# Experts' low-rank output in two float32r passes, with the feed-forward's vector steps in a new order

## The reference

```python
RANKS = (8, 16, 32, 64); TOPK = 1; SCALING = 1.0 / 4
base = x @ W.T + b                      # W [512, 512]
gate = x @ gate_w.T + gate_b            # 4 logits; the best of the four ranks is chosen
lora = (x @ A.T)                        # A [64, 512]; the columns up to the chosen rank are kept
x = _layernorm(x + base + lora_kept @ B.T)   # B [512, 64]
```

## Time and profile before

| | |
|---|---|
| Median of three runs | 645.35 us |
| The profiled execution's own time | 645.23 us |
| Its span | 643.1 us, so 2.1 us lie around it |
| Granted clock of PE | 0.998 |
| Busy: PE, DVE, ACT, POOL | 632.0, 396.3, 381.6, 65.0 us |

### The profile page before, as it was taken

One profiled execution on the slowest core, in us unless ns is written; L12 is line 12 of the kernel. 1 busy time (PEld: TensorE's weight loads), 2 busy tenths in 40 slices (PEclk: granted clock), 3 DMA queues, 4 the chain that ended last, 5 costly groups with the idle time before them and its releaser, 6 DMA issues.

```text
span 643.1 us, 8521 instructions
## 1 busy us (share of the span) xinstructions
PE 632.0 (98%) x3226; PEld 470.0 (73%) x3226; DVE 396.3 (62%) x633; ACT 381.6 (59%) x527; POOL 65.0 (10%) x116
## 2 busy tenths in 40 slices
PE   9999999999999999999999999999999999999996
PEld 6655555544558888888888888887777888888874
DVE  4798787667988777767667355335655212125467
ACT  2977789976987697576675154223565343316532
POOL 1032142311330000000000000001211000000012
PEclk9999999999999999999999999999999999999999
DMA  7771585512253134233320003056010322100002
GB/s 246 288 243 52 188 268 172 162 52 92 81 152 120 39 110 139 73 104 111 94 83 2 1 1 131 1 216 274 1 33 2 115 77 88 33 1 0 1 33 99
DMA packets 25590, 63.92 MB, mean 99 GB/s; under 512 B 5541, under 2 KB 10725, under 8 KB 24782
## 3 DMA queue, kind: packets, MB, share of 16 engines
q1 hardware_dynamic: 23294, 61.68, 29.4%
q10 hardware_dynamic: 2256, 1.70, 0.8%
HBM read 58.77 MB, written 4.60 MB: 99 GB/s over the span
## 4 chain that ended last, share of the span: by engine, by line
PE 88%; DVE 4%; ACT 4%; DMA 1%; issue 1%; SPq 1%; POOL 0%; POOLq 0%; DVEq 0%; ACTq 0%
PE bank L1043 18%; PE bank L1031 8%; PE bank L1030 8%; PE bank L1032 8%; PE bank L1122 8%; PE bank L1121 8%; PE bank L882 4%; PE bank L802 3%; PE bank L606 3%; PE bank L741 2%; PE bank L1097 1%; DMA codes<-in_c_qkv 1%; PE bank L912 1%; PE bank L926 1%; PE bank L984 1%
## 5 line engine op out<-in xcount | busy, mean ns | idle before, releaser
L1232 ACT ACTIVATE line<-line 128x1024 f32<-128x1024 f32 x87 | 91.4, 1050 | 0.2
L1030 PE MATMUL bank<-xh,wh 128*128 128x512 f32 x224 | 87.5, 391 | 0.0
L1031 PE MATMUL bank<-xl,wh 128*128 128x512 f32 x224 | 87.5, 391 | 0.0
L1032 PE MATMUL bank<-xh,wl 128*128 128x512 f32 x224 | 87.3, 390 | 0.0
L1043 PE MATMUL bank<-wh,xh 128*128 128x512 f32 x192 | 76.1, 396 | 0.2 <-DVE xl L2128 0.2
L1043 PE MATMUL bank<-wh,xl 128*128 128x512 f32 x192 | 74.9, 390 | 0.0
L2211 DVE SCALAR_TENSOR_TENSOR arena<-bank,ff_s,arena 128x512 f32<-128x512 f32 x28 | 21.0, 752 | 72.9 <-PE bank L1122 63.8
L2128 DVE TENSOR_TENSOR xl<-arena,xh 128x1024 fp32r<-128x1024 f32 (+1 forms) x26 | 29.7, 1141 | 35.4 <-ACT xh L1536 35.3
L1121 PE MATMUL bank<-xh,wh 128*128 128x512 f32 x128 | 50.3, 393 | 0.0
L1536 ACT ACTIVATE xh<-arena 128x1024 fp32r<-128x1024 f32 (+1 forms) x26 | 25.6, 991 | 41.3 <-PE bank L1043 34.8
L1122 PE MATMUL bank<-xl,wh 128*128 128x512 f32 x128 | 49.9, 390 | 0.0
(11 more groups left out here) (219 smaller groups left out, 1264.3 us busy)
## 6 DMA issues: line engine op xcount, KB each, us to landing
codes<-in_c_gu SPq DMA_DIRECT2D x14, 512.0 KB, 3.8
scales<-in_s_gu SPq DMA_DIRECT2D x28, 256.0 KB, 4.0
codes<-in_t_gu SPq DMA_DIRECT2D x8, 512.0 KB, 4.2
codes<-in_c_dn SPq DMA_DIRECT2D x7, 512.0 KB, 4.6
scales<-in_s_dn SPq DMA_DIRECT2D x14, 256.0 KB, 3.9
fold<-in_t_dn SPq DMA_DIRECT2D x1, 3584.0 KB, 15.7
codes<-in_c_qkv SPq DMA_DIRECT2D x6, 512.0 KB, 4.8
scales<-in_t_gu SPq DMA_DIRECT2D x6, 512.0 KB, 3.8
```

The costliest lines, as they stand in the source:

```text
L1030: pe.matmul(dst, wh[:, s, c:c + P], xh[:, k, cols], start=(k == 0), stop=False)
L1031: pe.matmul(dst, wh[:, s, c:c + P], xl[:, k, cols], start=False, stop=False)
L1032: last = pe.matmul(dst, wl[:, s, c:c + P], xh[:, k, cols], start=False, stop=(k == KD - 1))
L1232: nc.scalar.activation(below(slot), below(slot), ACT.Prelu, bias=bias, scale=scale, alpha=alpha).then_inc(bent, 1)
```

## The change

`lora_out` is two float32r products in place of one float32 product. The first has 128 rows: the stationary operand `lm_both` holds the low parts of the 64 masked columns in rows 0 to 63 and their high parts in rows 64 to 127, and `b_both` holds B's high part in rows 0 to 63 and B's low part in rows 64 to 127. The second has 97 rows: the high parts against B's high part, and two rows of ones against b's high and low parts. Its ones are written once on ACT.

For that `choose` makes two more DVE instructions: a copy of the masked columns to float32r (the high part) and a subtraction (the low part), each of 128x64, and each waits for the one before it. `lora_T` turns 128 columns, and `lora_T_out` is two ACT instructions (128x128 and 64x128) in place of one of 64x128. B and b come as two tiles (`b_two`, 256 KB, and `b_one`, 97 rows) in place of `bT0` (130 KB); they are loaded later, in SP's loop at t = 4. ACT rounds them once (`experts_high`), and DVE makes their low rows once (`experts_low`, two instructions between `choose(0)` and `choose(1)`).

The steps are in a new order. On DVE a step is now: the `add_lora`s, part 0 of the units, the wait and `ln_head` of tile t, `choose` of tile t+2, `m_low_of`, `x_low` of tile t-2, then part 1 of the units. On ACT `lora_T_out` of tile t+1 stands behind `x_T_out` in step t, ahead of part 1 of the units, where that of tile t stood first in step t.

```diff
             def lora_out(b):
                 pe.wait_ge(lmT_ready, b + 1)
-                pe.matmul(bank[FF_BANK[b % 3]][:, :], lmT[0:RMAX + 1, b % 2, :], bT0[0:RMAX + 1, :], start=False, stop=True).then_inc(f0_ps, 1)
+                if b == 0:
+                    pe.wait_ge(lm_ready, 2)
+                pe.matmul(bank[FF_BANK[b % 3]][:, :], lm_both[:, b % 2, :], b_both, start=False, stop=False)
+                pe.matmul(bank[FF_BANK[b % 3]][:, :], lm_one[0:ONE_ROWS.stop, b % 2, :], b_high_one[0:ONE_ROWS.stop, :], start=False, stop=True).then_inc(f0_ps, 1)
...
-                nc.scalar.activation(lmT[0:RMAX, b % 2, :], turn_bank(b)[0:RMAX, P:2 * P], ACT.Copy).then_inc(lmT_ready, 1)
+                nc.scalar.activation(lm_both[:, b % 2, :], turn_bank(b)[:, P:2 * P], ACT.Copy)
+                nc.scalar.activation(lm_one[0:RMAX, b % 2, :], turn_bank(b)[RMAX:P, P:2 * P], ACT.Copy).then_inc(lmT_ready, 1)
...
-                nc.vector.tensor_tensor(lm[:, s, :].rearrange("p (r m) -> p r m", m=SEG), ps[:, 0:RMAX].rearrange("p (r m) -> p r m", m=SEG),
-                                        mask.unsqueeze(1).to_broadcast([P, RMAX // SEG, SEG]), ALU.mult).then_inc(lm_ready, 1)
+                chosen, high = lm[:, s, 0:RMAX], lm_high[:, s, RMAX:P]
+                link(nc.vector.tensor_tensor(chosen.rearrange("p (r m) -> p r m", m=SEG), ps[:, 0:RMAX].rearrange("p (r m) -> p r m", m=SEG),
+                                             mask.unsqueeze(1).to_broadcast([P, RMAX // SEG, SEG]), ALU.mult))
+                link(nc.vector.tensor_copy(high, chosen))
+                nc.vector.tensor_tensor(chosen, chosen, f32(high), ALU.subtract).then_inc(lm_ready, 1)
...
             for t in range(NT):
-                if t >= 3:
-                    x_low(2 * NT + t - 3)
...
                 if t == 4:
                     down_stack_low()
+                dve.wait_ge(f0_ps, t + 1)
+                ln_head(2 * NT + t, plus(FF_BANK[t % 3]))
                 if t + 2 < NT:
                     choose(t + 2)
                 if FIRST_M <= t < FIRST_M + KD:
                     m_low_of(t - FIRST_M)
-                dve.wait_ge(f0_ps, t + 1)
-                ln_head(2 * NT + t, plus(FF_BANK[t % 3]))
+                if t >= 2:
+                    x_low(2 * NT + t - 2)
```

More of the change, by code:

```diff
@@ L170, in decoder_kernel @@
         ad_st = sb("ad_st", [STACK, FF], F32R)
+        with nc.sbuf_tensor("lm_one", [P, T], F32R) as lm_one:
+            pass
         folded_m = sb("folded", [P, T])
@@ L188, in decoder_kernel @@
         gate_v = sb("gate_v", [P, 2, NL + 3 * SEG])
-        lmT = sb("lmT", [P, 2, P])
-        probT = lmT
+        with nc.sbuf_tensor("lm_both", [P, 2, P], F32R) as lm_both:
+            pass
+        probT = sb("probT", [P, 2, P])
         prob = sb("prob", [P, 2, P])
@@ L221, in decoder_kernel @@
         bT_d, at = carve(arena, at, D)
+        b_high_at = at
         wk2, at = carve(arena, at, D)
@@ L237, in decoder_kernel @@
         lora_l = wo0
+        b_two, b_one = wk3, m_free[:, 0:D]
+        b_both, b_high_one = arena_r[:, b_low_at:b_low_at + D], arena_r[:, b_high_at:b_high_at + D]
+        ONE_ROWS = slice(RMAX, RMAX + ROWG + 1)
+        lm_one = lm_one[:, 0:2 * P].rearrange("p (s t) -> p s t", s=2)
         ad_high = wh[:, :, :].rearrange("p s c -> p (s c)")[:, 0:FF]
@@ L546, in _ @@
                     load_codes(C_O + 1 + t // 2)
+                if t == KD:
+                    sp.dma_start(b_two, i["b_two"]).then_inc(in_ffn0, 16)
+                    sp.dma_start(b_one[0:ONE_ROWS.stop, :], i["b_one"]).then_inc(in_ffn0, 16)
             load_scales(C_O + NT // 2)
@@ L1384, in _, with experts_high @@
             unit_bends(NT, 1)
+            def experts_high():
+                act.wait_ge(in_ffn0, 64)
+                nc.scalar.activation(b_both, b_two, ACT.Copy)
+                nc.scalar.activation(b_high_one[0:ONE_ROWS.stop, :], b_one[0:ONE_ROWS.stop, :], ACT.Copy).then_inc(stack_hi, 1)
             for t in range(1, NT + 2):
+                if t == NT + 1:
+                    experts_high()
                 if 2 <= t < NT:
@@ L1459, in _ @@
                     m_high_of(t - FIRST_M)
-                for u, h in half_plan(3, t, 1):
-                    unit_bends(u, h)
-                if t == 1:
+                if t == 2:
                     for n in range(2):
@@ L1466, in _ @@
                     x_T_out(2 * NT + t - 2, dst=xh)
+                if t + 1 < NT:
+                    lora_T_out(t + 1)
+                for u, h in half_plan(3, t, 1):
+                    unit_bends(u, h)
                 if t < 2:
@@ L2009, in _ @@
             turn_norm(2 * NT - 1)
+            experts_low()
             choose(1)
@@ L2304, in layout @@
         "w0T": rows(c(f["L0_ffn_W"].T)), "agT": rows(np.concatenate([f["L0_ffn_A"][rank_at].T, np.stack([gate_w[n] for n in LOGITS], 1)], 1)),
-        "bT0": np.concatenate([f["L0_ffn_B"].T[rank_at], f["L0_ffn_b"][None]]), "g_b": np.array([[gate_b[n] for n in LOGITS]], np.float32),
+        "b_two": np.concatenate([f["L0_ffn_B"].T[rank_at]] * 2),
+        "b_one": np.concatenate([f["L0_ffn_B"].T[rank_at], f["L0_ffn_b"][None], np.zeros((ROWG - 1, D), np.float32), f["L0_ffn_b"][None]]), "g_b": np.array([[gate_b[n] for n in LOGITS]], np.float32),
         "c_qkv": pairs(ca[:3].reshape(3 * KD, P, D)), "c_o": pairs(ca[3].T.reshape(KD, P, D)),
```

29 lines of the change are left out of this document (18 added, 11 removed).

## The result

The changed kernel takes 646.25 us, the median of seven runs (646.02 to 648.57). The kernel before took 645.35 us beside it (644.33 to 645.71). The ratio is 1.0026 with a 95% interval of 1.0016 to 1.0036: slower, by about as much as a measurement of this kernel can tell. The forecast was 646.5. The prediction had put nearly the same chance on no change (0.50) and on slower (0.44), with the border at 0.2% or 1.3 us; the result lies close to that border, and the interval reaches over it. The profiled execution took 646.25 us, its span is 644.4 us.

What follows compares the result with a forecast made beforehand. PE bounds the kernel with hardly any reserve on DVE. PE saves 3.3 us but waits some 4.5 us more, so 1.2 us later: 646.5 on the 645.35 median; the forecast's own range is 646.1 to 647.0, the stated range 645.0 to 648.0.

Steps and rivals of the forecast that it cites:

- What PE saves: `lora_out` on PE: two passes of 0.23 us replace 0.87, saving 0.41 us a tile, 3.3 us for eight.
- What DVE is given: Each `choose` on DVE gains a dependent copy and subtraction: 0.49 us each, 3.9 us for eight.
- the walk: Following DVE through its new order with old start distances, to see whether PE's 3.3 us survive: 1.2 us later.
- Stretch A: From the sum of tile 0 (137.82) to the first `attention_product` (156.90): 0.53 us late.
- Stretch B: From the sum of tile 3 (162.10) to the last `m_low_of`'s end (188.15): `attention_out` 1.64 us late at first.
- PE's waits: PE idle before `ffn_W(4)`, `ffn_W(5)`, first `attention_product`, tile 4's turn (about 2 us), `attention_out`; some 4.5 us more.
- Edits at no cost: `experts_low`, `experts_high`, ones and loads fall into idle time; `lora_T_out` copies add 0.17 us a tile on ACT, covered.
- (a): Rival: DVE's order hides its additions and PE's gain is kept, 642.1 us; chance 0.06.
- (b): Rival: DVE's added pair costs 0.35 us, not 0.49, so 645.7 us, no change; chance 0.22.
- (c): Rival: DVE's added pair costs up to 0.64 us, 647.4 us; chance 0.20 with the dearer pass.
- (d): Rival: ACT becomes last, its added copies lengthening DVE's loop in six tiles, 1.0 us more, 647.5 us; chance 0.06.
- three passes of 0.41: Range's end: a float32r pass costs as much as a float32 one (0.43), losing PE's gain at three places: 647.8.

Runs made afterwards that it cites:

- e3: Changed kernel without the copy and subtraction in each choice, low part of the masked columns left out: 644.66 us, ratio 0.9990.
- e4: Changed kernel with the 128x64 copy of each choice made twice: 649.30 us, ratio 1.0066.
- e5: Changed kernel with only the plan's list of weight units per step altered for feed-forward's first seven tiles: 643.58 us, ratio 0.9978.
- e1: Changed kernel with the two passes and split kept, but DVE's and ACT's steps back in the old order: 648.66 us, ratio 1.0056.
- e7: Changed kernel without the first of its two passes (lm_both against b_both), DVE's and ACT's work kept: 647.04 us, ratio 1.0038.
- e8: The changed kernel itself, measured again with nothing altered: 647.21 us, ratio 1.0033.
- e2: Kernel before, float32 product kept, with only DVE's and ACT's steps in the new order: 645.63 us, ratio 1.0004.
- e9: Kernel before, float32 product kept, with the new order of steps and the altered list of e5: 644.42 us, ratio 0.9990.

## Why the prediction was right, step by step

*What PE saves: the right term, sized somewhat too high.* The passes take 0.24 to 0.25 us each between float32 instructions (137.39 and 137.64) and 0.23 between float32r ones (191.25 and 191.48). Against 0.87 that is 0.37 to 0.39 us a tile where seven tiles stand among float32 work, and 0.41 for the eighth. From the start of a `ranks` to the start of the turn behind `lora_out` it is 1.75 us before (136.27 to 138.02) and 1.36 now (136.35 to 137.71), 0.39 a tile: 3.1 us in all in place of 3.3.

*What DVE is given: very nearly as taken.* The copy has a mean of 196 ns over eight and the subtraction 225. The step from `choose`'s first row to the next work is 1.29 us, 0.07 less than the 1.36 (0.87 + 0.49) of the walk. The 0.87 held a short wait: the sum behind that choice, at 138.22, could not start before `lora_out(0)` had ended at 138.19. The other choices of the kernel before take 0.81 to 0.83 us, and now 1.28, so that 0.46 are added and not 0.49. e3 and e4 show that this price is what decides. The pair was bounded by 0.35 and 0.64 us; it is 0.43 plus two handovers, and from 140.11 (L1995) the next starts follow after 0.26 and 0.23. The copy's 196 ns agree with the 0.19 us that I estimated from the Trainium skill's page "VectorE: DVE Perf Modes" (sections "The perf-mode tier table (the rule you actually need)" and "The TRN2 errata — SBUF-src ops pay a fixed extra latency per instruction").

*Stretch A: right.* The sum of tile 0 started at 137.91 (walk: 137.82), the first `attention_product` at 156.92 (156.90). The new trace starts 0.08 us later than the old one by `ranks(0)`, and without that it is 137.83 and 156.84.

*Stretch B: right.* The sum of tile 3 started at 162.24 (162.10), the last `m_low_of` ended at 187.47 + 0.66 = 188.13 (188.15), and `attention_out` started at 188.19 (188.20). Its second product is at 188.53 against 186.79 before: 1.74 late (1.64). Behind `lora_out(7)` the next `attention_out` is 1.34 late, so 0.40 is given back (0.41). That it fits to 0.1 us is in part luck, since small misses cancel: the stretch began 0.14 us late, DVE then took 25.89 us in place of 26.05 (three additions of 0.46 in place of 0.49, and a last `m_low_of` of 0.66 in place of 0.69), and the first product of `attention_out` is a record of 0.50 us where the walk had 0.39.

*PE's waits: right in sum, one place unforeseen.* I named four places and `attention_out`; the one ahead of `lora_out(6)`, for ACT's `lm_one`, was not among them. It was no loss of its own: in the walk PE stands still until DVE's `x_low` anyway, and the wait behind it is 1.60 where I had said about 2.

*Edits at no cost.* `experts_high` lies in ACT's idle time ahead of the first turned tile, of which 2.19 us of 3.23 are left. The ones don't, as I had taken it: their row starts at 132.37, behind the copy of that tile, and lasts 0.50 us. They cost nothing all the same, for the first `lora_T_out` behind them starts at 132.89 and `lora_out(0)` at 137.16, without a wait. On DVE `experts_low` starts at 129.59, and it and `choose(1)` leave 0.58 us of the 4.20. The two loads issue at 107.59 and 108.05, and the next issue of SP is at 111.46 against 111.38 before. Only `lora_T_out` was under-priced. ACT in order of time, beside the earlier trace rows:

```profile
131.75 0.60 ACT L1289 ACTIVATE arena<-bank 128x512 f32<-128x512 f32 x1 [2.19 <-PE bank L618]
...
181.22 0.27 ACT L1474 ACTIVATE lm_one<-bank 64x128 fp32r<-64x128 f32 x1
181.40 2.13 ACT L1247 ACTIVATE line<-line 128x1024 f32<-128x1024 f32 x2
```

Its first copy starts at 180.93 and the second at 181.22, 0.29 later and not 0.18, in this tile as in the others: the second doesn't overlap the first. That adds 0.31 us a tile in place of 0.17 (0.29 and 0.18 against the 0.16 of the one copy before, 187.26 to 187.42). A further 0.12 us are lost where the next reader of a bank is `m_high_of`: it starts 0.83 us behind the `norm_tail` ahead of it (171.04 to 171.87), and before the change 0.72 (176.56 to 177.28). The second copy reads rows 64 to 127 of its bank, the others start at row 0; see the last section. ACT was idle for 2.2 us from 160 to 180, so that it was covered, as forecast, until `lora_out(6)` had to wait for it.

*The rivals.* (a), PE's gain kept, was wrong for this kernel, and is reached in part only by e5, where DVE's work lies at other times. (b) and (c) fall with the measured price of the pair. (The upper end of the range, 647.8 by three passes of 0.41, is 647.7 by its own terms; nothing hangs on it.) (d), ACT as the last, is wrong at the changed kernel but the next in line, as e3 shows. What no case held is the granted clock: it adds 1.4 us in one profile of the changed kernel, and the upper end of its runs (648.57) lies over my range, though the median doesn't.

What stays open in part: why e1's runs (648.44 to 649.73, beside the profiled 648.0) and e7's (up to 651.39) spread above their profiled executions. Both have a wait of 1.3 to 1.8 us ahead of the turn of tile 4, and both profiles show the full clock in the stage. The mean granted clocks of the other executions show that it fell in some of them: in e7 0.990, 0.992 and 0.994 in three of ten, the two slowest among them, against 0.999 in the profiled one; in e1 0.994 to 0.997 in the four others against 0.999. Where in the span it fell in them no trace shows, and e5's profile has a fall at 36 us, far from the stage.

## What to carry to other kernels

Work taken off the fullest engine is worth only what the second one lets through: here 3.1 us off PE became 1.25 us more, since the edit paid for them with 0.43 us and two handovers per tile on an engine that ran 25 us without idle. Before splitting a product, follow that engine from one idle time to the next, and count its additions there. And when such an engine is late in one step and idle in another, move work that has no deadline between the steps before calling the edit useless: the same edit with another list of units went from 0.26% slower to 0.2 to 0.4% faster.

## What was not expected of the hardware

- A wait costs PE more than its idle time says. The idle time counts from the end of the record before, but the first record behind a wait is longer than what the same product holds the queue for in the chain: `lora_out`'s first pass 0.50 us against 0.25, the turn 0.63 against 0.44, the first `attention_product` 3.70 against 3.43, `attention_out` 0.50 against 0.23, and `ffn_W` only 3.70 against 3.63. With the short wait at 188.19 the idle time is 3.64 us, and these differences (0.07 twice, then 0.27, 0.25, 0.19 and 0.27) add 1.1: 4.8 us of delay. That closes the sum: 4.8, less 0.4 for the one wait before, less the 3.1 that the passes save, is 1.3 us, against 1.25 measured.
- The granted clock can be at 1.2 GHz for some 3 us behind a wait of 1.59 us, and stay at 2.4 GHz behind the same wait in another execution of the same kernel (e8 and the first profile after). What PE did before it was the same: in the 2 us ahead of the turn it was busy for 0.41 us where the clock fell and 0.40 where it didn't, and in the 2 us before those for 1.41 and 1.43. e7's profile kept the full clock behind a longer wait, 1.83 us. So neither the length of the wait nor the work before it tells by itself, in these traces, whether the clock falls.
- On ACT an instruction that waits for nothing mostly starts some 0.1 us before the end of its predecessor. The copy that reads rows 64 to 127 of a bank doesn't: it starts 0.29 us behind the first copy, whose record is 0.28 (180.93 and 181.22). Nor does the next reader of a bank behind it, which starts at row 0 again: `m_high_of` starts 0.82 to 0.84 us behind a `norm_tail` of 0.80 in the kernel after, e1 and e3, which all have that copy, and 0.70 to 0.72 in the kernel before, e2 and e9, which don't. So the cost goes with a change of the first partition that is read; that this is the reason, and not another property of the copy, no run separates.
